# GpSimd makes the marks of the ranking phase, in four buffers of its own

## What is computed

```python
h = relu(layernorm(x)); x = x + gaussian_mixture_conv(h, edges, edge_attr)   # L0
h = relu(layernorm(x)); x = x + two_mean_sage_convs(h, edges)                # L1
h = relu(layernorm(x)); x = x + spline_convs(h, edges, edge_attr)            # L2
h = relu(layernorm(x)); x = x + two_sum_sage_convs(h, edges)                 # L3
# each sum over edges:  segment_sum(message[src], dst, num_segments=N)
```

## Time and profile before

| | us |
|---|---|
| median of three runs | 11395.62 (11379.77 to 11412.15) |
| span of the profiled execution | 11414.2 |
| DVE busy in it | 5543.8 |
| POOL busy in it | 6528.7 |
| all ranking copies (line 226), DVE | 259.8 (122.8 for r and c1, 55.5 for d, 81.5 for c2) |
| all ranking marks (line 232), DVE | 102.2 (49.5 for r and c1, 21.9 for d, 30.8 for c2) |

### The profile page before, as it was taken

How to read it: one execution, slowest core, us unless ns; L and a number is a source line. 1 busy time by engine, 2 the same in 40 slices (tenths; PEclk the granted TensorE clock), 3 DMA queues, 4 the chain that set the end, 5 groups by cost and what they waited for, 6 DMA issues and landing times. The chain is left out here.

```text
span 11414.2 us, 177920 instructions
## 1 busy us (share of the span) xinstructions
PE 6127.3 (54%) x45373; PEld 4965.7 (44%) x45374; DVE 5543.8 (49%) x10403; ACT 2324.9 (20%) x6224; POOL 6528.7 (57%) x6578
## 2 busy tenths in 40 slices
PE   5200066665777766666554646555555555554655
PEld 1100035553666664544444434334444444443444
DVE  9300075555555548888763536741111333383535
ACT  0000024442333321111004050011111111125050
POOL 0677737775677777777406060047777777756060
PEclk9555587787555558787556565565555555556565
DMA  9960012221433321111737475662000111126465
GB/s 367 199 61 5 14 44 84 82 83 50 117 102 101 100 73 51 53 54 49 145 94 246 84 261 127 140 52 27 13 13 8 27 28 28 25 53 255 98 252 104
DMA packets 1406964, 1074.85 MB, mean 94 GB/s; under 512 B 959771, under 2 KB 1258287, under 8 KB 1395302
## 3 DMA queue, kind: packets, MB, share of 16 engines
q1 hardware_dynamic: 1012260, 637.37, 24.3%
q0 software_dynamic: 239808, 283.02, 8.0%
q10 hardware_dynamic: 154752, 152.84, 4.4%
HBM read 553.89 MB, written 595.41 MB: 101 GB/s over the span
## 5 line engine op out<-in xcount | busy, mean ns | idle before, releaser
L2507 POOL DMA_INDIRECT msg<-msg,idx x1792 | 1743.1, 973 | 585.8 <-issue 531.7
L2337 POOL DMA_INDIRECT cell<-rec,idx x1008 | 1003.3, 995 | 1027.4 <-ACT rec L2325 737.0
L666 DVE TENSOR_TENSOR oh<-iota_f,rd 128x512 bf16<-128x512 f32 (+1 forms) x1261 | 824.8, 692 | 1379.1 <-PE ps L2259 1083.6
L979 POOL DMA_INDIRECT run_rows<-rec,idx x704 | 728.7, 1035 | 1274.7 <-ACT rec L962 1105.5
L2061 POOL DMA_INDIRECT cell<-rec,idx x1008 | 1073.6, 1065 | 421.3 <-issue 305.8
L1738 POOL DMA_INDIRECT rec_d<-rec,idx x880 | 907.2, 1031 | 453.8 <-issue 266.5
L397 POOL DMA_INDIRECT rec_r<-sc_rec,sc_idx x832 | 816.2, 981 | 596.5 <-ACT sc_rec L388 317.4
L2487 PE MATMUL ps<-w_stn,hft 128*128 x1792 | 600.1, 494 | 397.6 <-ACT hft L2441 389.6
L2274 PE MATMUL ps<-h_rows,oht 128*128 x2016 | 481.6, 403 | 583.3 <-ACT oht L2281 582.9
L1053 PE MATMUL ps<-got,oh 128*128 128x33 bf16 x12096 | 599.0, 197 | 334.7 <-DVE oh L666 319.0
L948 PE MATMUL ps<-planes,hot 128*128 x5632 | 493.2, 265 | 516.1 <-ACT rec L962 406.9
(11 more groups left out here) (416 smaller groups left out, 13529.0 us busy)
## 6 DMA issues: line engine op xcount, KB each, us to landing
loc<-loc_s SPq DMA_DIRECT2D x88, 2048.0 KB
got<-run_rows SPq DMA_DIRECT2D x1008, 112.0 KB
got<-rec_d SPq DMA_DIRECT2D x252, 416.0 KB
rec_d<-padd ACTq DMA_DIRECT2D x4, 13312.0 KB
rec_d<-padd ACTq DMA_DIRECT2D x4, 12896.0 KB
cell<-rec,idx POOLq DMA_INDIRECT x2016
loc<-loc_d SPq DMA_DIRECT2D x252, 128.0 KB
cin<-cell SPq DMA_DIRECT2D x224, 136.0 KB, 2.2
```

Source lines behind the costliest of these rows:

```text
L666: return nc.vector.tensor_tensor(oh, bcast(iota_f[:, :].unsqueeze(1), [P, G, P]), bcast(local.unsqueeze(2), [P, G, P]), ALU.is_equal)
L979: nc.gpsimd.indirect_dma_start(out=out, out_offset=bass.IndirectOffsetOnAxis(ap=idx[:, u, m % HU:m % HU + 1], axis=0), in_=rec[:, m, :], i ...
L2337: nc.gpsimd.indirect_dma_start(out=cells, out_offset=bass.IndirectOffsetOnAxis(ap=idx[:, n, g:g + 1], axis=0), in_=rec[:, n, g, :], in_off ...
L2507: nc.gpsimd.indirect_dma_start(out=msgs, out_offset=bass.IndirectOffsetOnAxis(ap=idx[:, n, g:g + 1], axis=0), in_=msg[:, n, g, :], in_offs ...
```

## The change

POOL gets a program for the ranking marks in all three blocks that sort (`mark_pool`, for r and c1 one behind the other). It makes them from the same key and the same column of `iota_f`, as the same comparison, into four new buffers `again`, and counts them in a new counter `remarked`. It starts when the first mark of the counting phase is made, since the key is then there; from the fifth on it waits for the copy of four bins back. DVE's ranking loop is left with the copies alone, which read `again`. PE's ranking loop waits for `remarked` and reads `again`. The counting phase stays as it is, and its marks stay on DVE.

```diff
+        def mark_pool(pool, c, key, bins):
+
+            again = c["again"]
+            pool.wait_ge(c["marked"], 1)
+            for b in range(bins):
+                if b >= len(again):
+                    pool.wait_ge(c["kept"], b - len(again) + 2)
+                nc.gpsimd.tensor_scalar(again[b % len(again)][:, :], key, iota_f[:, b:b + 1], None, ALU.is_equal).then_inc(c["remarked"], 1)
+
         def keep_ranks(v, then, c, key, bins, tiles, row_out):
 
-            marks, rank, pos, lane, half = c["marks"], c["rank"], c["pos"], c["lane"], c["rank"].shape[1] // 2
-
-            def keep(b):
+            again, rank, pos, lane, half = c["again"], c["rank"], c["pos"], c["lane"], c["rank"].shape[1] // 2
+            for b in range(bins):
                 v.wait_ge(c["ranked"], b + 1)
                 v.wait_ge(c["kept"], b + 1)
-                nc.vector.copy_predicated(halves_of(rank[:, :]), halves_of(marks[b % 2][:, :].bitcast(I16)),
+                nc.vector.copy_predicated(halves_of(rank[:, :]), halves_of(again[b % len(again)][:, :].bitcast(I16)),
                                           ps[:, 4 + 2 * (b % 2):6 + 2 * (b % 2), 0:half]).then_inc(c["kept"], 1)
-
-            for b in range(bins):
-                if b >= 2:
-                    v.wait_ge(c["kept"], b)
-                nc.vector.tensor_scalar(marks[b % 2][:, :], key, iota_f[:, b:b + 1], None, ALU.is_equal).then_inc(c["marked"], 1)
-                if b:
-                    keep(b - 1)
-            keep(bins - 1)
...
         def rank_pe(pe, c, bins):
...
-                pe.wait_ge(c["marked"], bins + b + 1)
+                pe.wait_ge(c["remarked"], b + 1)
...
-                    nc.tensor.matmul(at, c["before_b"][:, :], marks[b % 2][:, h * half:(h + 1) * half], start=True, stop=False)
+                    nc.tensor.matmul(at, c["before_b"][:, :], again[b % len(again)][:, h * half:(h + 1) * half], start=True, stop=False)
...
+            s["again"] = [sb_in(c, f"again{n}", [P, cols], BF16) for n in range(4)]
...
+                    mark_pool(pool, srt["r"], key_b[:, :], 50)
+                    mark_pool(pool, srt["c1"], key_b[:, :], CELLS)
...
+                        mark_pool(pool, w, key[:, :], NB)
...
+                        mark_pool(pool, w, key_b[:, :], CELLS)
```

More of the change, by code:

```diff
@@ L276, in rank_pe @@
         def rank_pe(pe, c, bins):
-            marks, half = c["marks"], c["rank"].shape[1] // 2
+            again, half = c["again"], c["rank"].shape[1] // 2
             pe.wait_ge(c["carried"], 1)
             for b in range(bins):
-                pe.wait_ge(c["marked"], bins + b + 1)
+                pe.wait_ge(c["remarked"], b + 1)
                 if b >= 2:
@@ L340, in sort_own @@
             s["tbi"], s["tba"] = sb_in(c, "tbi", [P, MQ], I32), sb_in(c, "tba", [P, MQ], I32)
-            s.update({k: sem_in(c, k) for k in ("marked", "counted", "kept", "spread", "summed", "carried", "ranked",
+            s.update({k: sem_in(c, k) for k in ("marked", "remarked", "counted", "kept", "spread", "summed", "carried", "ranked",
                                                 "mapped", "stored")})
@@ L733, in _ @@
                         rank_pe(pe, w, NB)
+                    @block.gpsimd
+                    def _(pool):
+                        mark_pool(pool, w, key[:, :], NB)
                     @block.vector
```

## The result

| | before | after |
|---|---|---|
| median, us | 11395.7 (11379.8 to 11412.2, four runs) | 11591.9 (11558.2 to 11638.5, four runs) |
| span of the profiled execution, us | 11414.2 | 11636.4 |

The ratio is 1.0181, with an interval of [1.0162, 1.0199]; the medians differ by 196 us (1.0172, inside that interval). The prediction had 11366 us and a range up to 11470. The profiled execution of after is its slowest run, so its span shows more than the medians do.

The account below looks back on a forecast made before the run. DVE was taken to bound the rankings, with gains only in d and c2, as the fill covers r and c1: -35 us for marks off DVE, +5 for counting, so 11395.6 - 30 = 11366 us, range 11350 to 11470.

Parts of the forecast that it names:

- DVE is the bound, and a mark off it is on the path in d and c2: Ranking of d and c2: DVE has no gap and ends the block, so removing its marks saves 14 and 21 us.
- The copy's pitch of 1.24 and 1.37: Ranking of d and c2: copy behind copy takes 1.24 and 1.37 us a bin, against 1.54 and 1.71 now.
- The forecast of -14 and -21: Rankings of d and c2, L217 to last copy: 47 x 0.30 and 62 x 0.34 us saved, together -35 us.
- The price of POOL's mark: Ranking marks on POOL: 1.06 ns an element, 1.05 us at 880 columns and 1.19 at 1008, under the copy's pitch.
- the break-even of 1.64: Ranking in d and c2: at 1.64 ns an element on POOL, the change neither gains nor loses time.
- POOL is slower than DVE was: Rival, all four sorts: at 2.1 ns an element POOL's marks set the pitch, +100 us, 11496 us; chance 0.16.
- the cover: First block (r, c1): ACT's fill of rec_d ends it, so gains count nothing and losses show beyond 2.9 us.
- PE stays hidden and its clock stays: Ranking in c2: PE needs 1.03 us within the copy's 1.37, 0.3 us to spare at full clock; no clock fall.
- the argument from the busy share: PE in c2's ranking: 66.2 of 108 us busy held clock 0.98, and the share grows, so no fall expected.
- Mutual exclusion of copy and mark: Rival, ranking: DVE's copy and POOL's mark take turns, some +165 us, 11565 us with the counting; chance 0.11.
- Four marks in the counting phase: Counting phases of d and c2: POOL's early marks cost DVE 0 to 9 us, taken as 5 us.
- 0.08 and a quarter of 0.50: Chance of faster by over 0.3%, given as 0.22: the 35 to 42 us gain plus a quarter of the forecast.

Follow-up runs that it names:

- The last experiment: Against the kernel before: r and c1 unchanged; in d and c2 POOL makes odd marks, ACT even ones, DVE only copies; ratio 0.9966, 33 us less.
- the split in all four sorts: Against the kernel before: in all four rankings POOL makes the odd marks and DVE the even ones, POOL starting with the ranking; ratio 0.998.

## Why the prediction was wrong

**DVE is the bound, and a mark off it is on the path in d and c2: right.** The last experiment takes exactly this away and gains 30.2 us in the two blocks.

**The copy's pitch of 1.24 and 1.37: right.** 1.25 and 1.39 were measured in long rows; the pair of copies at the end of a sort was a good witness. The forecast of -14 and -21 for the two is met from L217's end to the last copy: -13.7 (75.7 to 62.0 us) and -19.8 (109.9 to 90.1). The whole blocks gained 11.9 and 18.3; most of the difference lies ahead of L217, where POOL's first marks stand beside DVE's small steps (in c2 one of 0.25 us, which writes `diag`, lasts 0.91) and each block is 1.3 us longer than before from its key to L217.

**The price of POOL's mark: this step failed.** The prediction bounded it by 0.83 ns an element (iota) and 2.1 (subtraction), with 3.6 as the worst, and took 1.06, half the two-input price, "as if the reads set it". It is 2.50 ns and 0.29 us fixed, beyond both the break-even of 1.64 and the two-input price, which I had treated as a ceiling of a quiet POOL. The choice rested on a reason (one input, half the reads) for which no row spoke. The row of the same kind of work, an elementwise operation of an ALU, was the subtraction, and it was also the nearest in price; iota reads and compares nothing. The page "GPSIMD Engine Reference" of the Trainium skill, section Engine selection, which has one-input operations at about line rate, holds here for COPY (1.03 us) and not for TENSOR_SCALAR (2.80 us). Its section Performance pitfalls for Q7 kernels has 2.03 cycles an element for one form of such a body and 1.03 for the other. By an estimate from the first the mark is just above the break-even, and by the second it is below the forecast's 1.06 ns; the runs, with 2.50 ns, have it above both.

**The rival "POOL is slower than DVE was": it came true, mis-sized.** At 2.1 ns it gave 11496 us. Its own sum at the measured price is close: +43 and +66 for d and c2 with the ready marks and the counting about cancelling, and +99 - 10.7 for r and c1, together 197, against 196 measured. By the blocks it was 42.3, 66.0 and 82.8. So the structure of the sum held; that its total comes within 1 us is luck, since the first block's term is over 5 us high (DVE ended 93.6 us later and not 99). Its chance of 0.16 and the upper end of 11470, which cut it in half, did not.

**The first block: the cover is real, its thickness wrong.** Gains there are worth nothing (the split in all four sorts), losses show from 10.7 us on and not from 2.9. The step that was mis-sized here read the wait of SP as the room and left out that the map DMAs in that tail get faster once the fill is over.

**PE stays hidden and its clock stays: half right.** PE was the bound only at the very start of a ranking (7551.94 to 7553.62 above, 1.68 us, which is no more than today's pitch, as the prediction had it). But its clock fell: 0.52 over c2's ranking in after, 0.50 in its steady part. PE did the same four matmuls per bin, at 0.60 to 0.63 us each, then waited 0.92 us for POOL. Before, it waited 0.68 us in 1.71 at 0.98. Its busy share was even higher (113.9 of 170 us against 66.2 of 108), so the argument from the busy share was no argument: longer matmuls make the share. With marks in time it is 0.96 and 0.98. It cost nothing in the steady loop, because POOL's 2.78 us hide 1.9 us of slow PE.

**Mutual exclusion of copy and mark: rejected.** Copies last 1.28 us beside POOL in after, and POOL's mark 2.80 us beside copies. The Trainium skill ("SBUF — State Buffer", Who interferes with whom) leaves such a copy free of POOL, and here the trace agrees.

**Four marks in the counting phase: size right, by luck.** DVE's timeline of d, counting phase, with POOL's four marks:

```profile
1524.11 0.92 DVE L748 CAST key<-rec_s 128x880 bf16<-128x880 f32 x1 [15.46 <-DMA map_i<-map_r]
...
1525.62 10.62 POOL L226 TENSOR_SCALAR again<-key,iota_f 128x880 bf16<-128x880 bf16 x4 [23.09 <-DVE mark L203]
...
1527.99 2.19 DVE L203 TENSOR_SCALAR mark<-key,iota_f 128x880 bf16<-128x880 bf16 x3 [0.28 <-PE ps L272]
1530.49 2.27 DVE L203 TENSOR_SCALAR mark<-key,iota_f 128x880 bf16<-128x880 bf16 x3 [0.30 <-PE ps L272]
...
1557.28 1.99 DVE L247 TENSOR_TENSOR_SCAN seen<-ones,total 128x880 f32<-128x880 f32 x1
```

From the key's cast to the scan behind the counting it is 33.17 us, and 30.59 before: +2.58 in d. By the same rows it is +3.65 in c2 (43.19 and 46.84), together 6.2 where 5 was forecast. That 5 was a bit over half of 8 x 1.1 = 9 us of POOL's time; the eight marks really took 22.6 us (10.6 and 12.0), of which DVE lost about a quarter. Two wrong sizes cancelled. Three marks of DVE in 2.2 us are about 0.73 each instead of 0.45, and DVE got thirteen of them done in POOL's 10.6 us. So the two slow each other but do not shut each other out for the whole of an instruction; the section of the Trainium skill that says so of a fast mode is not borne out, for by it the cost would have been near the 22.6 us of the eight marks.

**The chances** have a slip of their own: 0.08 and a quarter of 0.50 are 0.205 and not 0.22. Nothing hangs on it.

## What to carry to other kernels

Before work moves to another engine, price it by a row of the same kind of instruction on that engine; an iota, a fill or a copy is no witness for arithmetic, and where the only alike row lies above break-even, take that row and not an average with a cheap one. A slow helper may still be of use if it gets only the share that its own time allows, one mark in two here, and a third engine the rest. And the room under a cover is measured from the engine's end to the block's end; parts of that tail may be slow only because of the cover itself. Last, a change that brings both a helper and more buffers has two causes of gain, and the buffers alone are the cheaper one to try.

## What the runs showed of the hardware

- On POOL a TENSOR_SCALAR of 128x1008 takes 2.80 us, more than a TENSOR_TENSOR of two f32 tensors (2.31), and a COPY 1.03. The ALU operation, the type and the kind of scalar hardly count (2.73 to 2.81).
- POOL's mark and DVE's fast bf16 mark slow each other (2.80 to 3.17 us, and from 0.47 to up to 1.39 us), as do POOL's mark and a two-input subtraction on DVE (3.32 us, and the subtractions 1.21 and 1.99 in turn). A masked copy from PSUM and POOL's mark don't (1.28 and 2.80).
- In after TensorE's granted clock stood at 0.50 in the steady loop of c2, in which it waited 0.92 us of each 2.78. It stood at 0.98 in before, with 0.68 us of each 1.71, and in the last experiment, with 0.34 and 0.41 us in turn of each 1.39.
- One indirect DMA of `run_ids` takes 26.5 and 34.4 us in two of seven profiled executions. What makes it so stays open.
